# An RWKV, FFN and attention block on one core: every engine's order within a tick rewritten, attention and second FFN moved against the first

## The reference, cut to what matters

```python
x = x + rwkv(layernorm(x))      # 4 layers, each time mixing and channel mixing
x = x + ffn(layernorm(x))       # fp4 quantised, gate and up of width 352, silu
x = x + attention(layernorm(x)) # one causal head of width 64
x = x + ffn(layernorm(x))       # the same FFN once more

# one RWKV layer
h = layernorm(x); hh = time_shift(h)
k, v, r = Wk @ mix(h, hh), Wv @ mix(h, hh), sigmoid(Wr @ mix(h, hh))
x = x + Wo @ (r * wkv(k, v))            # wkv: a scan over the 512 tokens
h = layernorm(x); hh = time_shift(h)
x = x + sigmoid(Wcr @ mix(h, hh)) * (Wcv @ square(relu(Wck @ mix(h, hh))))

# the FFN
gate, up = q(x) @ q(w_gate).T, q(x) @ q(w_up).T
return q(silu(gate) * up) @ q(w_down).T   # q: fp4 in blocks of 16
```

## Time and profile before

| | us |
|---|---|
| median of three runs | 1396.85 |
| span of the profiled execution | 1396.8 |
| tensor engine busy | 1311.6 |
| scalar engine busy | 1261.8 |
| vector engine busy | 1250.5 |
| gpsimd busy | 1160.8 |

### The profile page before, as it was taken

The page is one execution under the profiler, slowest core; times in us unless marked ns, Lnnn a source line. Parts: engine busy times, 40 slices in busy tenths (PEclk is TensorE's granted clock), DMA queues, the critical chain, the costliest instruction groups (busy, mean ns, idle before and its releaser), DMA issues.

```text
span 1396.8 us, 23610 instructions
## 1 busy us (share of the span) xinstructions
PE 1311.6 (94%) x7285; PEld 929.9 (67%) x7285; DVE 1250.5 (90%) x2169; ACT 1261.8 (90%) x2533; POOL 1160.8 (83%) x1218
## 2 busy tenths in 40 slices
PE   3699999999999999999999999999999999999997
PEld 1356667666666666676666677766667777667776
DVE  6999999999999999999999999579999467789994
ACT  6799999999999999999999999767777889888874
POOL 6888999999998999998998999969998445467983
PEclk9999999999999999999999999999999999999999
DMA  7000000000000000000000000100000000000011
GB/s 232 0 1 1 1 1 1 1 20 13 1 1 1 1 1 1 1 1 1 1 2 0 1 1 9 31 24 23 24 1 1 1 1 1 1 8 23 24 31 38
DMA packets 26924, 18.55 MB, mean 13 GB/s; under 512 B 1072, under 2 KB 26160, under 8 KB 26800
## 3 DMA queue, kind: packets, MB, share of 16 engines
q1 hardware_dynamic: 26800, 17.05, 4.2%
HBM read 12.85 MB, written 4.19 MB: 12 GB/s over the span
## 4 chain that ended last, share of the span: by engine, by line
ACT 40%; PE 30%; issue 11%; POOL 10%; DVE 8%; DMA 0%; ACTq 0%; SPq 0%; POOLq 0%; DVEq 0%
ACT z L757 10%; ACT kf L867 6%; PE ps L1211 5%; ACT kf L874 3%; PE ps L1190 3%; ACT rc L841 3%; PE ps L1152 3%; ACT ed L818 3%; PE ps L1183 3%; PE ps L1261 3%; PE ps L1135 3%; ACT er L835 2%; PE ps L1243 2%; ACT ed L819 2%; ACT ed L830 2%
## 5 line engine op out<-in xcount | busy, mean ns | idle before, releaser
L1152 PEld LDWEIGHTS ps<-W,kf 128*128 128x128 f32 x2048 | 245.9, 193 | 33.1 <-issue 32.3
L1135 PE MATMUL ps<-xk,W 128*128 128x512 f32 x512 | 262.5, 595 | 1.0 <-DVE xk L404 0.9
L1152 PE MATMUL ps<-W,kf 128*128 128x128 f32 x2048 | 251.2, 276 | 0.0
L757 ACT ACTIVATE z<-X,ln_rs 128x128 f32<-128x128 f32 x512 | 219.2, 720 | 6.1 <-POOL ln_rs L606 6.1
L867 ACT ACTIVATE kf<-ps 128x512 f32<-128x512 f32 x256 | 210.8, 823 | 3.5 <-PE ps L1135 3.5
L874 ACT ACTIVATE kf<-kf 128x1024 f32<-128x1024 f32 x128 | 164.7, 1287 | 0.0
L1040 PEld LDWEIGHTS ps<-idn,z 128*128 128x128 f32 x664 | 81.1, 143 | 113.7 <-issue 68.4
L1040 PE MATMUL ps<-idn,z 128*128 128x128 f32 x664 | 101.9, 277 | 32.8 <-ACT z L757 19.4
L604 POOL TENSOR_TENSOR ln_rs<-ln_rs,mhalf 128x8 f32<-128x8 f32 (+1 forms) x70 | 122.9, 1756 | 0.0
L707 POOL TENSOR_TENSOR W<-W,hsc 128x704 f32<-128x704 f32 x64 | 88.9, 1389 | 30.3 <-DVE hsc L482 30.3
L666 POOL TENSOR_TENSOR p<-p,rc 128x512 f32<-128x512 f32 x64 | 104.2, 1628 | 8.6 <-DVE p L381 8.0
(11 more groups left out here) (178 smaller groups left out, 4041.5 us busy)
## 6 DMA issues: line engine op xcount, KB each, us to landing
X<-x_in SPq DMA_DIRECT2D x16, 256.0 KB, 6.8
xi<-x_in SPq DMA_DIRECT2D x16, 256.0 KB, 2.8
out<-X SPq DMA_DIRECT2D x16, 256.0 KB, 2.3
W<-weights SPq DMA_DIRECT2D x4, 832.0 KB, 8.4
W<-fp4w SPq DMA_DIRECT2D x1, 560.0 KB, 3.6
row<-rows SPq DMA_DIRECT2D x1, 192.0 KB, 2.9
wqkv<-qkv SPq DMA_DIRECT2D x1, 96.0 KB, 5.9
idn<-ident SPq DMA_DIRECT2D x1, 64.0 KB, 3.0
```

The source lines that it names most:

```text
L757: last = e.activation(chunk(dst, j), chunk(src, j), ACT.Identity, bias=rs[:, 1, j:j + 1], scale=rs[:, 0, j:j + 1])
L1135: e.matmul((pF0, pF1)[f % 2][:, :], w_of(r, WCK + f), xk[r % 2][:, :], start=True, stop=True).then_inc(kf_mm[f], 1)
L1152: last = e.matmul(chunk(pKV, j), kf[r % 3][:, f, j * 128:(j + 1) * 128], w_of(r, WCV + f), start=f == 0 and j == 0, stop=f == 3, skip_grou ...
```

## The change

It keeps every instruction and every semaphore. It rewrites the four lists of steps, with new lags, and the three constants: attention starts 15 ticks after the first FFN, the second FFN 29 ticks after it, and the loop has 133 ticks where it had 131. The `if` of `ffn_job` names its own bound, since ATT_AT no longer lies at the end of the first FFN. The lags of the gpsimd list are two to three ticks larger throughout; as engines are tied only by semaphores, a shift of a whole list moves no step against its neighbours in that list.

```diff
-GAP = 12
-ATT_AT, FFN2_AT, TICKS = FFN_AT + NB, FFN_AT + NB + GAP, FFN_AT + 2 * NB + GAP + 18
+ATT_AT, FFN2_AT = FFN_AT + 15, FFN_AT + 29
+TICKS = FFN2_AT + 35
...
-            return t - FFN_AT if FFN_AT <= t < ATT_AT else t - FFN2_AT + NB if FFN2_AT <= t < FFN2_AT + NB else None
+            return t - FFN_AT if FFN_AT <= t < FFN_AT + NB else t - FFN2_AT + NB if FFN2_AT <= t < FFN2_AT + NB else None
```

Lags of the other stages that the prediction speaks of:

```diff
-                weights_scales(t - Q_AT)
+                weights_scales(t - Q_AT + 4)
...
-                silu(ffn_job(t - 6), 3)
...
-                silu(ffn_job(t - 5), 0)
...
-                a_exp(att_job(t - 6), 0)
...
-                a_exp(att_job(t - 6), 3)
...
-                silu(ffn_job(t - 5), 1)
...
-                silu(ffn_job(t - 5), 2)
...
+                a_exp(att_job(t - 6), 0)
...
+                a_exp(att_job(t - 6), 3)
...
+                silu(ffn_job(t - 5), 1)
...
+                silu(ffn_job(t - 5), 2)
...
+                silu(ffn_job(t - 5), 3)
...
+                silu(ffn_job(t - 4), 0)
```

More of the change, by code:

```diff
@@ L533, in vector @@
             for t in range(TICKS):
+                mul_u(t - 8)
+                sub_d(t - 6)
+                rwkv(t - 8)
+                fx_add(ffn_job(t - 4))
+                mul_up(ffn_job(t - 6), 0)
+                a_add(att_job(t - 8))
+                bn1(t - 3)
+                arg_r(t - 6)
+                fx_inverse(ffn_job(t - 3))
+                mul_up(ffn_job(t - 6), 1)
+                weights_rounded(t - Q_AT - 2)
+                init_stats(t - 1)
+                fx_sub(ffn_job(t - 4))
@@ L544, in vector @@
[L544 to L556, removed]
@@ L557, in vector @@
-                weights_scales(t - Q_AT)
-                a_mask(att_job(t - 6), 1)
-                mul_rv(t - 6)
+                fh_max(ffn_job(t - 6))
+                prepare(t - 2)
+                mix_t(t - 5)
+                a_bn(att_job(t - 2))
+                fh_add(ffn_job(t - 7), 1)
+                fh_scale(ffn_job(t - 6))
+                fx_max(ffn_job(t - 2))
+                mix_rt(t - 5)
+                mix_r(t - 11)
+                add_xa(t - 8)
+                init_affine(t - 2)
@@ L986, in scalar @@
             for t in range(TICKS):
[L987 to L997 removed]
+                exp_k(t - 6)
                 keep_pt(att_job(t - 7), 0)
[L999 removed]
@@ L1034, in tensor @@
+                relu(t - 10, 2)
+                keep_hq(ffn_job(t - 7), 0)
+                a_z(att_job(t - 2))
+                fh_magic(ffn_job(t - 6), 1)
+                weights_out(t - Q_AT - 14)
+                silu(ffn_job(t - 4), 0)
+                keep_h1(t - 3)
+                keep_hq(ffn_job(t - 7), 1)
+                keep_x(ffn_job(t - 8))
+                args(t - 5)
+                exp_r(t - 5)
         def tensor():
@@ L1283, in tensor @@
                 p_turn(att_job(t - 7), 2)
-                ff_values(t - 12, 0)
+                p_turn(att_job(t - 7), 3)
+                lend_T(t - 6)
+                output(t - 8)
+                receptance(t - 6)
+                ff_values(t - 12, 1)
+                ff_keys(t - 10, 0)
+                ff_keys(t - 10, 1)
                 similarity(att_job(t - 6), 2)
-                lend_T(t - 6)
-                a_keys(att_job(t - 5))
-                p_turn(att_job(t - 7), 3)
-                ff_keys(t - 11, 3)
+                keys(t - 5)
```

181 lines of the change are left out of this document (84 added, 97 removed).

## The result

The change makes the kernel slower: 1415.64 us in the median of four runs (1415.25 to 1415.72) against 1396.71 for the kernel before in the same comparison (1395.51 to 1397.21), a ratio of 1.0134 [1.012, 1.0149]. The forecast was 1391.5. The profiled execution spans 1413.8 us, 17.0 more than before's 1396.8.

The account below looks back on a forecast made before the run. The scalar engine was taken to bound the RWKV part, tensor work plus table-load excess the ticks shared by attention and second FFN. Stages -3.3, start -1.0, fp4 weights -1.0 sum to -5.3: 1396.8 to 1391.5 us, range 1381 to 1402.

Parts of the forecast that it names:

- Everything else I cost at nothing: Remaining moves, including both FFN ticks: 0, as the full gpsimd and vector lists keep their instructions.
- New orders, same work: Middle RWKV part: reordered lists with unchanged work leave the tick at 13.2 us, nothing faster.
- Start: Kernel start, prepare(0) ahead of init_affine(0): 3.3 us late weights, 1.65 and 2.6 given back, -1.0 us; ends -4 to +3.3.
- RWKV ticks: Some 50 ticks bound by the scalar engine: 0 us, ends -1 to +3.
- the feared 0.04 us of `exp_k`: Scalar list of an RWKV tick: new wait of exp_k behind args and exp_r, only 0.04 us of room.
- fp4 weights: Between 700 and 800 us: weight preparation spread out takes off scalar idle time, -1.0 us, ends -3.2 and +1.
- The spread I counted on: weights_scales and weights_rounded six ticks apart instead of two, letting the vector engine, with 3.6% to spare, recover between.
- Stages: Attention and second FFN shifted: four of 13 table loads go, two shared ticks instead of four, -3.3 us; ends -10.2, +1.4.
- the 16.84: Tensor work in us of a full shared tick, also the cost of one attention tick moved over the first FFN's tail.
- the spread ticks: Attention and second FFN ticks that run apart instead of shared: 7.68 + 9.88 = 17.56 us for a pair.
- Slower, by the start: Rival: weights land late, +3.3 us, plus +2 from exp_k's wait over 50 ticks: 1401.1 us; chance 0.20.
- its stage gain: In the slower rival, a smaller gain of 1 us from the shifted attention and second FFN, taken off its +5.3.

Follow-up runs that it names:

- experiment 13: Kernel after with fx_scale behind fx_max, init_affine ahead of mix_k, prepare at its old place and lag, and add_res in its old tick: 1401.37 us, 1.0034.
- experiment 12: Kernel after with fx_scale behind fx_max, and init_affine, prepare and weights_rounded directly ahead of scan_bb: 1402.52 us, 1.0034.

## Why the prediction was wrong

- **The step that failed** is "Everything else I cost at nothing", with its reason "both keep their instructions", and the same thought in "New orders, same work". I took an instruction's duration as a property of the instruction. The rows of before that would have spoken were there (L259 in its groups at 235 ns on average, where most took 0.17), and I had read GpSimd for its load and not for what it meets. The second FFN tick, which I called full, went from 9.88 to 10.56 us, and moving one line away from L707 gave 8.4 us.
- **Start**, forecast -1.0. The weights came late as costed (+2.65 us at `init_affine(0)`, forecast +3.3), and `add_xa(0)` came 1.8 us early, within the ends. But I had stopped at the chain's first job. VectorE bounds the start's ticks (49.90 us of 50, ScalarE 44.99), and +10.7 us follow by job 20. Moving `init_affine` alone produces such a loss in the kernel before; in after it is `init_affine` and `mix_r` together.
- **RWKV ticks**, forecast 0: 343.0 us for 26 ticks against 343.2, and the feared 0.04 us of `exp_k` didn't come. The holding is there as well (L337 at 779 ns instead of 479, 19.3 us in all), but ScalarE sets this tick, and VectorE's room paid for it: its busy time went from 331.5 to 343.0 us in these 26 ticks. That is one part of why 51.8 us more of busy time made only 17.0 us more of span; the other stretches used up idle time of VectorE as well.
- **fp4 weights**, forecast -1.0: between `add_xa` 46 and 56, 135.6 became 139.9 us, +4.3. The spread I counted on gave VectorE no rest, as its room was used up by then (343.0 us busy of 343.0 just before). In the ticks behind it, `gated` was held in six, and in two once `add_res` stood in its old tick again (experiment 13), a move that I had costed at nothing too.
- **Stages**, forecast -3.3: nine loads as counted. The size was neither right nor wrong by itself: 0.0 with the old lists, -7 with the new ones. My sum left out the first-FFN tick that the 16.84 replace and a second-FFN tick that then runs alone; the two nearly cancel. Redone by stretch it is 16.84 - 151.2 / 15 = +6.8 us in the first FFN and 37.7 + 17.56 + 9.88 - 75.4 = -10.3 in the last stretch. With the old lists +6.9 and -6.0 came: the first term was right, and the spread ticks gave back less than costed. With the new lists the last stretch gave -10.8. From `keep_x(0)` on, after takes +2.2 us against before, and with `fx_scale` moved -4.3.
- **The rivals.** "Slower, by the start" had the sign and a place, and a mechanism (late weights, 2 us) that carries little of it. With its stage gain it came to +4.3 us, less than a quarter of the loss. None of the rivals had VectorE's instructions grow longer.

Open: what the best kernels still lack (in experiment 12, 4.9 us from `add_xa` 0 to 20 and 8.6 from 46 to 63, of which what follows returns 10.0), what decides the clock drop, and why L259 on hsc<-ham is never held (232 ns in before, 229 in after) where the same operation on xsc is. The two differ in more than being in place: ham is read as 11 rows of 8 out of rows of 9, xsc as 32 elements in a row, and no run changes either.

## What to carry to other kernels

When a hand-written order is redrawn, lay VectorE's and GpSimd's instructions side by side in every kind of tick, and mark each vector instruction with two inputs in SBUF, and each TENSOR_SCALAR from SBUF to SBUF until a trace shows it free. Beside a GpSimd product its price is what remains of that product and then its own time, not its own length alone. Put there what reads PSUM, bn_stats, or a reduction, and remember that a moved step pushes its neighbours into the same place. Holding cost nothing where another engine set the tick (the RWKV ticks here), so look for it first where VectorE is at 100%.

## What the hardware showed that I had not expected

- An instruction of 0.17 us on 32 elements a partition took 1.02 us beside a 1.39 us GpSimd product, ending with it. The wait is to the end of the other instruction, not a slowdown of both.
- GpSimd waits as well, where the VectorE instruction began first: L666 took 1628 ns on average in before and 1356 in after. The change took 17.4 us off GpSimd at this line and gave 51.8 to VectorE in all.
- The clock fell to 1.2 GHz for some 6 us in one tick, and not in a kernel with the same waits ahead of it; the tick took 19.1 us instead of 16.1.
